# Four chained layers on one core: residual sums on the matrix engine, normal forms from PSUM, and a new order of a round

## The reference, cut to what matters

```python
x = _layernorm(x + L0_attn(x))   # L0_attn ends in  out @ W_out + b_out + x
x = _layernorm(x + L0_ffn(x))    # top-2 of 8 experts, 128x128 each, softmax gate
x = _layernorm(x + L1_attn(x))   # 16 heads of 8, softmax features, causal linear attention, y @ w_out.T
x = _layernorm(x + L1_ffn(x))    # batch norm over all tokens, product keys, top 8 of 8192 rows of down and up
```

## Time and profile before

| what | us |
|---|---|
| median of three runs | 583.02 |
| lowest, highest | 580.79, 585.88 |
| profiled execution, its own time | 583.85 |
| its span, first to last instruction | 582.1 |
| set-up and batch 0 of `a` | 0 to 67 |
| joint rounds | 67 to 129.6, to 191.4, to 253 |
| last round and the end of layer 3 | 253 to 311.3 |
| `peer()` | 311.3 to 582 |

### The profile page before, as it was taken

How to read it: one execution, slowest core, us unless ns; L and a number is a source line. 1 busy time by engine, 2 the same in 40 slices (tenths; PEclk the granted TensorE clock), 3 DMA queues, 4 the chain that set the end, 5 groups by cost and what they waited for, 6 DMA issues and landing times. The chain is left out here.

```text
span 582.1 us, 12503 instructions
## 1 busy us (share of the span) xinstructions
PE 411.8 (71%) x4564; PEld 293.6 (50%) x4564; DVE 482.1 (83%) x2076; ACT 314.8 (54%) x643; POOL 182.2 (31%) x208
## 2 busy tenths in 40 slices
PE   1778868987999699956746345868657675855575
PEld 0555447644765477625642123546445353724475
DVE  4576869699869987898963998799979999989991
ACT  0601376418542664236421639586786868588590
POOL 4450133933194318613513132103030303030000
PEclk9987978797967986776556855775868585958576
DMA  7210000000000000000000000000000000000000
GB/s 213 78 46 0 1 2 2 1 2 0 2 1 2 1 1 2 2 0 1 2 1 0 1 1 1 3 2 11 3 11 1 11 3 9 3 10 2 11 2 19
DMA packets 12459, 6.72 MB, mean 12 GB/s; under 512 B 3182, under 2 KB 11758, under 8 KB 12398
## 3 DMA queue, kind: packets, MB, share of 16 engines
q1 hardware_dynamic: 10566, 4.34, 2.7%
q10 hardware_dynamic: 1832, 1.58, 0.8%
HBM read 4.87 MB, written 1.05 MB: 10 GB/s over the span
## 5 line engine op out<-in xcount | busy, mean ns | idle before, releaser
L1738 ACT ACTIVATE hot_last<-iota_f,lo_last 128x128 f16<-128x128 f32 x256 | 75.8, 391 | 0.3 <-DVE lo_last L1862 0.3
L2000 PE MATMUL psum<-hot_w,hot_lo 128*128 128x16 f16 x1536 | 43.3, 172 | 15.1 <-DVE hot_lo L1879 15.1
L1879 DVE TENSOR_TENSOR hot_lo<-lo_t,iota_lo 128x4096 f16<-128x4096 f16 x24 | 53.6, 2287 | 0.3
L1966 PE MATMUL psum<-x3t,down_t 128*128 128x512 f32 x64 | 43.8, 789 | 13.3 <-ACT hid L1704 11.6
L2000 PEld LDWEIGHTS psum<-hot_w,hot_lo 128*128 128x128 f16 x1536 | 41.7, 101 | 21.5 <-DVE hot_lo L1879 19.8
L1652 POOL TENSOR_TENSOR eq<-eq,side_f 128x1024 f16<-128x1024 f16 x14 | 28.9, 2083 | 55.5 <-DVE eq L1840 55.5
L1329 PE MATMUL psum<-q_hi,k_t 32*128 32x128 f16 x256 | 36.5, 260 | 9.1 <-DVE masked L905 7.9
L2000 PE MATMUL psum<-hot_w,hot_last 128*128 128x16 f16 x512 | 14.8, 174 | 38.7 <-issue 31.2
L1660 POOL TENSOR_TENSOR rstd<-rstd,minus_half 128x2 f32<-128x2 f32 x8 | 5.6, 702 | 115.0 <-DVE rstd L1909 115.0
L1809 DVE FIND_INDEX8 side_i<-side,keysims 128x8 uint32<-128x32 f32 x256 | 41.5, 185 | 0.0
L1250 PE MATMUL psum<-we,x1t 128*128 128x512 f32 x64 | 40.3, 777 | 0.4 <-DVE z L842 0.4
(11 more groups left out here) (271 smaller groups left out, 1194.5 us busy)
## 6 DMA issues: line engine op xcount, KB each, us to landing
xall<-in_L_attn_x SPq DMA_DIRECT2D x4, 256.0 KB, 6.2
out<-o SPq DMA_DIRECT2D x8, 128.0 KB, 2.8
we<-in_L_ffn_We SPq DMA_DIRECT2D x1, 512.0 KB, 4.3
downn<-in_L_ffn_down SPq DMA_DIRECT2D x1, 512.0 KB, 5.2
upw<-in_L_ffn_up SPq DMA_DIRECT2D x1, 512.0 KB, 6.3
wh<-in_L_attn_W_h SPq DMA_DIRECT2D x1, 256.0 KB, 4.2
keysn<-in_L_ffn_keys_p ACTq DMA_DIRECT2D x1, 256.0 KB, 9.4
wqkv<-in_L_attn_w_qkv ACTq DMA_DIRECT2D x1, 192.0 KB
```

The source lines that it names most:

```text
L1738: ins = nc.scalar.activation(hot_last[:, lane], iota_f[:], ACT.Abs, bias=lo_last[:, lane:lane + 1], scale=-1.0)
L1879: nc.vector.tensor_tensor(hot_lo[:, pairs], bc(lo_t[:, lanes].rearrange("p (j s) -> p j s", s=2).unsqueeze(2), [P, LB // 2, P, 2]), bc(v.i ...
L1966: nc.tensor.matmul(bank[H_BANK(b, c)][:], v.down_t[:, c, :], v.x3t[:, N * b:N * b + N], start=True, stop=True).then_inc(h_mm.h, 1)
L2000: ins = nc.tensor.matmul(bank[2 + q][:, c:c + 2 * EH], low, hot_w[:, i, lane // 2, :, :, lane % 2].rearrange("p t e -> p (t e)"), start=(i ...
```

## The change

Three things change in `layers()`; `peer()` is as it was.

1. Two residual sums go to PE. `a_out` adds `ident x xall` to each tile's two products, `b_z3` adds `ident x x2` to each tile's one. The tiles `z` and `z3`, DVE's `a_z` and `b_z3` and the semaphore z3_ok go. `a_z_spread`, `a_x1`, `b_z3_spread` and `b_x3` read PSUM banks 3 and 6. So a batch's `b_x3t`, which writes bank 6, waits for all four tiles of x3, but for the last batch, which gets bank 7 (`X3T_BANK`). `a_kv`, which writes bank 0, now also waits for ACT's first gate.
2. POOL's hold on x1_ok goes.
3. The loop is split into joint rounds (`for a in range(1, B)`, b = a - 1) and the last round written out, and in the joint rounds all four engines get another order. The last round keeps its order, except that DVE's `b_z3` is gone.

```diff
+    X3T_BANK = (6,) * (B - 1) + (7,)
...
@@ ScalarE @@
+                for a in range(1, B):
+                    b = a - 1
+                    a_val(a, 0)
+                    b_x2t(b, 1)
+                    a_val(a, 1)
+                    a_qk(a)
+                    b_maps(b, 1)
+                    b_exp(b, 0)
+                    a_heads(a)
+                    a_link(a)
+                    b_exp(b, 1)
+                    a_gate(a, 0)
+                    if b:
+                        b_x3t(b - 1)
+                    a_gate(a, 1)
+                    a_kv(a)
+                    b_features(b, 0)
+                    b_values(b, 1)
+                    b_value_head(b)
+                    b_features(b, 1)
+                    b_transposed(b, 0)
+                    b_transposed(b, 1)
+                    b_value_part(b)
+                    b_transposed(b, 2)
+                    b_transposed(b, 3)
+                    b_high_scores(b, 0, (0, 1))
+                    b_high_scores(b, 0, (2, 3))
+                    a_x1t(a)
+                    b_state_head(b)
+                    b_high_scores(b, 1, (0, 1))
+                    b_state_rest(b)
+                    a_exp(a)
+                    b_high_scores(b, 1, (2, 3))
...
+                    b_x2t(a, 0)
+                    b_maps(a, 0)
+                    b_values(a, 0)
                     b_yt(b)
...
@@ GpSimd @@
-                    if u == 0 and b + 1 < B:
-
-                        pool.wait_ge(x1_ok.h, T * (b + 2))
...
+                    if b:
+                        root(b_var, b_root, b_rstd, b - 1, 1)
                     b_negative(b, 0)
+                    a_heads(a, 3)
+                    a_heads(a, 1)
+                    b_negative(b, 1)
                     b_value_parts(b, 0)
                     b_value_parts(b, 1)
+                    root(a_var, a_root, a_rstd, a, 1)
+                    b_low_scores(b, 0, (0, 1))
+                    b_low_scores(b, 0, (2, 3))
+                    b_state_rest(b)
+                    b_low_scores(b, 1, (0, 1))
+                    b_state_low(b)
+                    b_low_scores(b, 1, (2, 3))
...
@@ VectorE @@
-                def a_z(b):
+                def a_z_spread(b):
 
                     wait(dve, out_mm, b)
-                    wait(dve, xres_ok, b)
-                    step(nc.vector.tensor_tensor(z[:], bank[3][:].rearrange("p (t d) -> p t d", t=T),
-                                                 v.xall[:, T * b:T * b + T, :], ALU.add))
-
-                def a_z_spread(b):
-
-                    spread_of(lambda u: z[:, u, :], a_stats, a_mv, a_rstd, a_var)
+                    spread_of(lambda u: bank[3][:, P * u:P * u + P], a_stats, a_mv, a_rstd, a_var)
...
-                    normal(lambda u: z[:, u, :], lambda u: x1[:, u, :], a_mv, a_rstd, x1_ok)
+                    normal(lambda u: bank[3][:, P * u:P * u + P], lambda u: x1[:, u, :], a_mv, a_rstd, x1_ok)
...
-                    nc.vector.tensor_tensor(z3[:], x2[:, b % 2], bank[6].rearrange("p (t d) -> p t d", t=T), ALU.add)\
-                        .then_inc(z3_ok.h, 1)
...
+                for a in range(1, B):
+                    b = a - 1
+                    if b:
+                        b_z3_spread(b - 1)
+                    a_x2(b, 1)
                     b_maps(b, 0)
+                    if b:
+                        b_x3(b - 1)
+                    b_maps(b, 1)
                     b_features(b, 0)
+                    a_attn(a)
+                    b_features(b, 1)
                     b_low_keys(b, 0)
+                    a_gated(a, 0)
+                    a_gated(a, 1)
+                    b_low_keys(b, 1)
                     b_low_queries(b, 0)
                     b_low_queries(b, 1)
+                    a_z_spread(a)
                     b_low_queries(b, 2)
                     b_low_queries(b, 3)
                     b_masked(b, 0, (0, 1))
+                    a_x1(a)
                     b_masked(b, 0, (2, 3))
+                    b_states(b)
+                    b_masked(b, 1, (0, 1))
+                    a_shift(a)
+                    b_masked(b, 1, (2, 3))
+                    a_choice(a)
+                    b_masked(b, 2, (0, 1))
+                    b_masked(b, 2, (2, 3))
+                    if b:
+                        b_moments(b - 1)
+                    b_masked(b, 3, (0, 1))
+                    b_summed(b, 0)
+                    b_summed(b, 1)
+                    b_masked(b, 3, (2, 3))
+                    a_experts(a, 0)
+                    a_z2(a, 0)
+                    b_summed(b, 2)
+                    b_summed(b, 3)
+                    a_x2(a, 0)
+                    b_y(b)
+                    a_experts(a, 1)
+                    a_z2(a, 1)
...
@@ TensorE @@
+                    wait(pe, gate_ok, b, 1)
...
                         for c in range(EC):
-                            ins = nc.tensor.matmul(bank[3][:, P * u:P * u + P], gated_t[:, c, P * u:P * u + P],
-                                                   v.wout0[:, c, :], start=(c == 0), stop=(c == EC - 1))
+                            nc.tensor.matmul(bank[3][:, P * u:P * u + P], gated_t[:, c, P * u:P * u + P],
+                                             v.wout0[:, c, :], start=(c == 0), stop=False)
+                        if u == 0:
+                            wait(pe, xres_ok, b)
+                        ins = nc.tensor.matmul(bank[3][:, P * u:P * u + P], ident[:], v.xall[:, T * b + u, :],
+                                               start=False, stop=True)
...
+                        nc.tensor.matmul(bank[6][:, P * u:P * u + P], yt[:, P * u:P * u + P], v.wout1_t[:],
+                                         start=True, stop=False)
+                        ins = nc.tensor.matmul(bank[6][:, P * u:P * u + P], ident[:], x2[:, b % 2, u, :],
+                                               start=False, stop=True)
...
+                for a in range(1, B):
+                    b = a - 1
+                    a_val(a, 0)
+                    a_val(a, 1)
+                    a_qk(a)
                     b_x2t(b, 1)
                     b_qkv(b, 1)
+                    if b:
                         b_x3t(b - 1)
+                    a_gate(a, 0)
+                    a_link(a)
+                    a_sim(a)
+                    a_gate(a, 1)
+                    a_kv(a)
+                    a_outt(a, 0)
+                    a_outt_linear(a, 0)
+                    a_outt(a, 1)
+                    a_outt_linear(a, 1)
                     b_transposes(b, 0)
                     b_transposes(b, 1)
+                    a_out(a)
                     b_transposes(b, 2)
                     b_transposes(b, 3)
+                    b_scores(b, 0, (0,))
                     b_products(b)
+                    b_scores(b, 0, (1,))
+                    a_x1t(a)
+                    b_scores(b, 1, (0,))
+                    a_logits(a)
+                    b_scores(b, 1, (1,))
+                    a_experts(a, 0)
+                    b_numerators(b, 0)
+                    b_scores(b, 2, (0,))
+                    b_scores(b, 2, (1,))
+                    b_scores(b, 3, (0,))
+                    b_numerators(b, 1)
+                    b_scores(b, 3, (1,))
+                    a_experts(a, 1)
+                    a_experts(a, 2)
+                    b_numerators(b, 2)
+                    b_numerators(b, 3)
+                    b_x2t(a, 0)
+                    a_experts(a, 3)
+                    b_qkv(a, 0)
                     b_z3(b)
```

More of the change, by code:

```diff
@@ L491, in b_x3t @@
                     wait(act, x3t_mm, b)
-                    nc.scalar.copy(v.x3t[:, N * b:N * b + N], bank[6][:]).then_inc(x3t_ok.h, 1)
+                    nc.scalar.copy(v.x3t[:, N * b:N * b + N], bank[X3T_BANK[b]][:]).then_inc(x3t_ok.h, 1)
                 def key_products():
@@ new lines, in _ @@
+                    a_experts(a, 0)
[6 more added lines that the diff above has]
+                    a_z2(a, 1)
+                b = B - 1
+                b_maps(b, 0)
+                a_x2(b, 1)
+                b_features(b, 0)
+                b_z3_spread(b - 1)
+                b_maps(b, 1)
+                b_x3(b - 1)
+                b_low_keys(b, 0)
@@ L1131, in _ @@
+                b_summed(b, 0)
+                b_masked(b, 3)
+                b_low_scores(3)
+                for u in range(1, T):
+                    b_summed(b, u)
+                b_y(b)
                 b_z3_spread(B - 1)
@@ L1481, in _ @@
                 key_products(1)
-                for s in range(1, B + 1):
-                    a, b = s, s - 1
-                    if a < B:
-                        a_val(a, 0)
-                        a_qk(a)
-                        a_gate(a, 0)
+                for a in range(1, B):
+                    b = a - 1
+                    a_val(a, 0)
+                    a_val(a, 1)
+                    a_qk(a)
                     b_x2t(b, 1)
```

(27 more changed lines are left out.)

225 lines of the change are left out of this document (68 added, 157 removed).

## The result

The changed kernel took 592.36 us, the median of four runs (589.49 to 593.98), beside 581.9 for the kernel before in the same comparison: a ratio of 1.0166, 95% interval 1.0096 to 1.0237. It is slower, by about 10 us. The forecast was 580.5 in a range of 568 to 591, and a small gain: the direction was wrong and the time lies outside the range. A second comparison of the same two kernels gave 1.0139 (1.0071 to 1.0207).

The account below looks back on a forecast made before the run. DVE's work in fixed order plus waits for PE and ACT bounds joint rounds. Rounds -3.2 - 0.5 - 0.5 = -4.2, set-up and last round +1.2, half-clock risk +0.4: -2.6, giving 580.5 us, range 568 to 591.

Parts of the forecast that it names:

- the walk: New engine lists laid side by side for round a=2, each step moved to its last input; five places make DVE wait.
- the middle: From a_gated(a,1) to b_low_queries(b,3), behind ACT's chain: DVE waits 2.55 us; masking starts at 26.05.
- Point 4: The scores: DVE waits 2.5 us, 0.5 for logits, 1.8 before masked(2), 0.2 more in tile 2's second half.
- Point 5: Before the experts, a_experts(a,1) behind the last scores: wait 0.35 at full clock, 2.1 at half, taken as 1.2 us.
- Point 1: Round's head, b_z3_spread first: PE needs 7.5 us, DVE has 6.6 to do; wait 1.0 us.
- Point 2: Before b_maps(b,1): pm is there at 6.45, DVE free at 5.3; wait 1.1 us.
- Sum of the waits: DVE's five waits in a steady joint round: 8.35 us against 6.8 before, +1.55.
- The first two rivals: PE at full clock through scores and experts, 571.5 us, chance 0.33; middle of round at half clock, 590.5, chance 0.16.
- signs of being wrong: A joint round under 59.5 or over 63 us, a PSUM normal form over 400 ns, or a change inside peer().
- The trade: Residual sums from DVE to PE: 1.0 us more on PE, 0.7 less on DVE; gain of 0.7 where DVE never waits.
- the fourth rival: The order does nothing, only the z sums show: 3 x -1.4 + 1.2, 580 us; no chance of its own given.
- The rival "full clock": PE at full clock through scores and experts saves 3.0 us a round: 571.5 us, chance 0.33.

Follow-up runs that it names:

- the fillers: Four unread fp32 512-column products per joint round added on PE: on the changed kernel 0.9993, with both moves 0.9883, on the kernel before 0.9879.
- both moves: Changed kernel with PE's a_experts(a,3) put back ahead of b_x2t(a,0) and a_experts(a,1) moved behind the first half of tile 2's scores: ratio 0.9944.
- e1: Kernel before, all engines in the old order, with only the residual sums on PE and statistics and normal forms read from PSUM: ratio 1.0096.

## Why the prediction was wrong

**The steps that held.** A single profile of round 2 gives, by the walk's own points: before b_maps(b,1) 0.50 (forecast 1.1); the middle 1.02 + 0.29 + 1.10 + 0.17 = 2.58 (forecast 2.55, item by item 0.6, 0.35, 1.4 and 0.2); masking at 25.9 us (26.05). The last round is 59.55 (59.4). Four table loads a round, without a drain. a_out took 2.90 us instead of 2.00 (forecast 3.0). In the last round two errors offset each other: z3's products grew by 1.47 (2.07 to 3.54) where 2.07 was taken, and the two longer b_x3 cost 0.5. POOL's hold on x1 was not tried by itself.

**The step that failed** is the length of PE's steps in points 4, 5 and 1, from the logits to the last expert product: they were taken at the full clock or at a mean of the two, and PE had 1.2 GHz. Point 4 (2.5) measured 2.78 + 0.53 = 3.3. Its expert product was priced at the half clock and rightly (3.55, measured 3.58 until the next step), but its two halves of scores, 0.8 and 0.45, were not: 1.36 until the expert product, and 1.12 from the start of the second until DVE could go on. Point 5 read "I take the middle, 1.2" and measured 0.48 + 0.36 + 2.19 = 3.0; its own price for the half clock, 2.1, was the right one. Point 1 had 1.0 ahead of b_z3_spread, where nothing was waited for; DVE waited 1.98 earlier, for tile 3's product, which took 3.29 where 1.9 was taken, and which the walk had set only against the whole pair of experts. Point 2 measured 0.6 less than forecast. Sum of the waits: 11.4 instead of 8.35. These 3.05 and 0.5 for the eight longer normal forms are nearly all of the 3.65 between the forecast 61.3 and 64.95. In the first round twelve waits make 13.8 instead of 9.7.

The earlier trace rows already showed that stretch at 0.53. The first two rivals had the clock as their subject, but one in the wrong direction and one in the wrong stretch: the middle kept 1.00. What I left out is the rival in which the half clock of the scores reaches the experts, with DVE queued directly behind each product. With the waits since measured, 2.0 + 3.0 + 3.3 in place of 1.0 + 1.2 + 2.5, it gives 3.6 a round, +10.9 - 2.6: 591.3 us. That sum is made afterwards; from the prediction's own prices only the 2.1 of point 5 was there. That the clock carries the loss is shown by the fillers: they alone bring the changed kernel from 1.0166 to 0.9993. Two of the prediction's own signs of being wrong showed: rounds over 63 us and a normal form from PSUM of 402 ns.

**The sums.** "The trade is a small loss wherever DVE waits for PE": right in sign, but the fourth rival had the sums alone gain 3 us, and alone in the old order they cost 1.0%, some 5 us. Part is the chain from a_out to tile 2's scores, on which DVE waits for PE and which I had not named (+1.07 in its longest wait besides the 1.65); the rest is not explained term by term. 0.25 us for the four PSUM forms of a_x1, set at nothing, is the smallest part. The Trainium skill's rule (VectorE: DVE Perf Modes, Why PSUM operands drop a tier) was right that they cost something; the measured 0.06 an instruction is half of the estimate of 0.13 worked out from its table.

**The rival "full clock"** put a round at 58.3. It did not happen by itself. With the fillers and both moves the rounds were 58.3 to 59.7 and, with z3 back on DVE, 58.6 to 59.6; in the changed kernel's own order the fillers held the clock only for seven to ten microseconds more, so the price in that rival fits what was measured but was not tried by itself.

**What stays open**: what decides which clock record peer() gets, and so how much of each ratio under 0.7% is that; whether holes or the lack of long products lower the clock in a round, and why it falls after 28 us in one round of the changed kernel and after 32 in the next; and the split of the 1% in e1.

## What to carry to other kernels

Where an engine waits on short steps of TensorE, price those steps at the clock that the trace grants in that stretch, and if two clocks are possible, walk the order once with each: the same product was 1.96 or 3.78 us here, and fillers that raised the clock took back the whole loss. An order by hand or by a search that feeds products just in time has no slack for the low clock; put the long products where they are early at 1.2 GHz. And before moving work off TensorE, try to give it some: four unread products in its holes were worth 0.6 to 1.7% in four orders of the round, of which the smallest gains are near what one kernel's times differ by.

## What the runs showed of the hardware

- The clock falls to 1.2 GHz while PE counts as busy for 10.78 of 11.00 us (before, 159.6 to 170.6, mean 0.55), and four 512-column fp32 products among the scores kept that stretch at 1.00, in this order (159.2 to 170.2 in its filled kernel) and in the new one. In the new order PE stood still for 2 of the 8 us ahead of the fall.
- The effect of a sum on PE depends on the order around it: z's sum there wins 1.0% in the order with both moves (1.0011 to 0.9912), and both sums cost 1.0% in the old order.
- A scaled difference of 128 fp32 columns takes DVE 402 ns from PSUM and 340 from SBUF. Four take 1.35 to 1.37 us from PSUM, with POOL at work or without; from SBUF 1.11 without and 1.70 beside POOL's work.
- The same program's profile differs in its first joint round by 1 to 2 us, with another clock record, and an untouched part of 270 us has two lengths 4 us apart, which differ in four of DVE's waits for PE.
